# In the last stage, the routing-weight matmul of a unit moves from in front of an older unit's down projection to behind it

## The reference, cut to what matters

```python
shared = silu(xf @ Ws_up) @ Ws_down
w = sigmoid(sel); w = w / (sum(w) + 1e-08)
cw = zeros((T, E)).at[arange(T)[:, None], idx].add(w)
h = silu(einsum('td,edf->etf', xf, W_up))
y = einsum('etf,efd->etd', h, W_down)
routed = einsum('etd,te->td', y, cw)
return shared + routed
```

## Time and profile before

| | us |
|---|---|
| median of 3 runs | 1024.24 |
| lowest and highest run | 1022.57, 1024.37 |
| the profiled execution, whole | 1021.6 |
| its span on the core | 1019.9 |
| TensorE busy in the span | 946.4 (93%) |
| VectorE busy | 825.4 (81%) |
| ScalarE busy | 700.0 (69%) |
| GpSimd busy | 480.2 (47%) |

### The profile page before, as it was taken

The page is one execution under the profiler, slowest core; times in us unless marked ns, Lnnn a source line. Parts: engine busy times, 40 slices in busy tenths (PEclk is TensorE's granted clock), DMA queues, the critical chain, the costliest instruction groups (busy, mean ns, idle before and its releaser), DMA issues.

```text
span 1019.9 us, 20123 instructions
## 1 busy us (share of the span) xinstructions
PE 946.4 (93%) x6082; PEld 754.9 (74%) x6115; DVE 825.4 (81%) x1938; ACT 700.0 (69%) x1394; POOL 480.2 (47%) x550
## 2 busy tenths in 40 slices
PE   3686999999789999999999979999999999999997
PEld 2564998999657677767776657787877777778786
DVE  6888776777778888888887668989898889898865
ACT  3763554555467777877787657777777778777875
POOL 3278782107456565656553404444444444444443
PEclk8765999999779999999999999999999999999999
DMA  8994332222201110110010008493939292939291
GB/s 258 403 386 167 109 95 67 69 66 69 60 24 28 30 29 23 29 33 24 22 32 12 1 16 197 97 210 82 213 76 220 72 222 66 213 76 219 70 228 42
DMA packets 69156, 111.00 MB, mean 109 GB/s; under 512 B 16783, under 2 KB 54706, under 8 KB 64962
## 3 DMA queue, kind: packets, MB, share of 16 engines
q1 hardware_dynamic: 64080, 100.72, 37.8%
q0 software_dynamic: 4384, 8.99, 2.8%
q10 hardware_dynamic: 594, 0.09, 0.0%
HBM read 70.90 MB, written 38.86 MB: 108 GB/s over the span
## 4 chain that ended last, share of the span: by engine, by line
PE 74%; DVE 16%; ACT 4%; issue 3%; DMA 1%; SPq 1%; DVEq 0%; POOLq 0%; ACTq 0%
PE ps L2494 6%; PE ps L2476 5%; PE ps L2477 5%; PE ps L2478 5%; PE ps L2495 5%; PE ps L2496 5%; PE ps L2199 3%; DVE nm L1919 3%; PE ps L2307 3%; PE ps L2329 3%; PE ps L2301 3%; PE ps L2346 3%; PE ps L2177 2%; PE ps L2179 2%; PE ps L2178 2%
## 5 line engine op out<-in xcount | busy, mean ns | idle before, releaser
L927 POOL TENSOR_TENSOR hl<-h,hh 128x512 fp32r<-128x512 f32 x128 | 166.8, 1303 | 247.8 <-ACT hh L1238 247.8
L1238 ACT ACTIVATE hh<-h 128x512 fp32r<-128x512 f32 (+1 forms) x264 | 165.4, 627 | 43.8 <-DVE h L2004 41.2
L2004 DVE TENSOR_TENSOR h<-ps,cwB 128x512 f32<-128x512 f32 x192 | 130.8, 681 | 31.0 <-ACT ps L1227 28.1
L1919 DVE TENSOR_REDUCE nm<-ps 128x4 f32<-128x512 f32 (+1 forms) x128 | 116.3, 951 | 38.0 <-PE ps L2329 35.9
L1227 ACT ACTIVATE ps<-ps 128x512 f32<-128x512 f32 x192 | 111.6, 581 | 25.6 <-PE ps L2478 24.8
L2476 PE MATMUL ps<-xh,wh 128*128 128x512 f32 x256 | 103.0, 403 | 0.0
L2494 PE MATMUL ps<-hh,wh 128*128 128x512 f32 x256 | 102.3, 400 | 0.6 <-POOL hl L927 0.6
L2011 DVE TENSOR_TENSOR hl<-h,hh 128x512 fp32r<-128x512 f32 (+1 forms) x136 | 95.9, 705 | 8.4 <-ACT hh L1238 8.1
L2495 PE MATMUL ps<-hl,wh 128*128 128x512 f32 x256 | 100.0, 390 | 0.0
L2477 PE MATMUL ps<-xl,wh 128*128 128x512 f32 x256 | 100.0, 390 | 0.0
L2478 PE MATMUL ps<-xh,wl 128*128 128x512 f32 x256 | 99.9, 390 | 0.0
(11 more groups left out here) (367 smaller groups left out, 2671.4 us busy)
## 6 DMA issues: line engine op xcount, KB each, us to landing
cwB<-cwd SPq DMA_DIRECT2D x32, 1536.0 KB, 13.8
ys<-zfill SPq DMA_DIRECT2D x13, 1536.0 KB, 22.6
cwd<-cwS SPq DMA_DIRECT2D x64, 96.0 KB
xb<-xs SPq DMA_DIRECT2D x72, 64.0 KB
ys<-yb SPq DMA_DIRECT2D x72, 64.0 KB
x_res<-in_L_attn_x_dram SPq DMA_DIRECT2D x4, 512.0 KB, 6.6
wst<-in_L_ffn_W_up_dram SPq DMA_DIRECT2D x32, 64.0 KB, 2.1
wst<-in_L_ffn_W_down_dram SPq DMA_DIRECT2D x32, 64.0 KB, 1.9
```

Of the source, the lines that this page charges most:

```text
L927: pool.tensor_tensor(hl4[:, slot(u), :], h4[:, slot(u), :], hh4[:, slot(u), :].bitcast(F32), op=ALU.subtract).then_inc(u_hlp, 1)
L1238: act.activation(hh4[r, slot(u), :], h4[r, slot(u), :], ACT.Copy).then_inc(u_hh, 1)
L1919: ins = dve.tensor_reduce(nm[:, u, 4 * g:4 * g + 4], o, axis=AX.X, op=ALU.max, negate=True)
L2004: dve.tensor_tensor(h4[:, slot(u), :], first, second, op=ALU.mult).then_inc(u_h, 1)
```

## The change

The spread matmul is taken out of `e_up` and made a function of its own, which `pe_tile` calls behind the down projection. Nothing else is altered: the same matmuls, the same waits, the same semaphores, in another order on TensorE alone.

```diff
@@ e_up
                 pe.matmul(o, lo, xh4[:, p, :], start=False, stop=True).then_inc(u_up, 1)
+
+            def e_spread(t, p, u):
                 if u > 0 and not broadcast_unit(u):
                     wait_bank(pe, t, "spread", u)
                     pe.matmul(bank[spread_bank(u)][:, :], selr[:, 2 * u - 2:2 * u, :].rearrange("p e f -> p (e f)"), cwT[:, p, :],
                               start=True, stop=True).then_inc(u_cw, 1)
@@ pe_tile
                         e_down(t, p, u - LAG)
                     elif before is not None:
                         e_down(before[0], 1 - p, NU + u - LAG)
+                    e_spread(t, p, u)
                     if before is None:
                         last_attended(u)
```

## The result

| | before | after |
|---|---|---|
| median of 6 runs, us | 1023.57 | 1019.93 |
| lowest and highest, us | 1021.67, 1024.37 | 1019.03, 1020.3 |
| ratio | | 0.9965, 95% interval 0.9954 to 0.9976 |
| profiled execution, us | 1021.6 | 1019.94 |
| its span, us | 1019.9 | 1018.2 |

The kernel became 3.6 us faster; 2.64 us were forecast, and the interval of the ratio (2.5 to 4.7 us of 1023.57) just takes them in. The span of the profiled execution fell by 1.7 us only: its last stage is 2.34 us shorter, but began 0.7 us later (608.67 us into the span against 607.97), behind code that is the same. From here on the spread matmul is L2483 and down is L2496 to L2498, since the edit puts two lines ahead of them.

A forecast was written before the change was run, and what follows sets the result against it. TensorE's row of matmuls in the last stage was taken to bound the kernel; gains of 0.66 + 0.11 + 0.22 + 0.48 + 0.48 + 0.69 = 2.64 us took 1024.24 to 1021.6 us, range 1019.5 to 1024.3.

The forecast's parts named there:

- The holes of unit 6: TensorE's spread matmul there waits for VectorE's late h of unit 4; 0.86, 0.11, 0.22, 0.57, 1.00, 0.57 us in tiles 0 to 5.
- The gain by tile: Last stage, tiles 0 to 5: gains of 0.66, 0.11, 0.22, 0.48, 0.69 and 0.48 us, summing to 2.64 us.
- The 0.09 us of restart kept in tiles 3 and 5: Unit 6: weights load one step ahead only at 769.95, so about 0.09 us stays and each tile gains 0.48 us.
- h at 1.33 us after the last up: Units 1 to 8: h would wait for the moved spread matmul, starting at 1.33 us instead of 1.23, 0.10 later per unit.
- The cap on tile 4: Unit 3's hole closes, but unit 6 arrives 0.63 us earlier at the same late h; tile gains 0.69 us, not 1.63.
- The cover: Units 1 to 8: down comes four units later, so h's 0.10 us delay doesn't add up; without it 6.4 us are lost.
- The loads of the weight rows: Before h of unit 9: the DMA never ended VectorE's idle time, so starting 0.6 us earlier should not find it late.
- The reading by which loads pass the wait: TensorE weight loads passing a waiting spread matmul would leave tiles 3 and 5 no restart; sum 2.82 us.
- VectorE's run of work: Rival: it slips by more than 0.10 us, delaying unit 7 in tiles 0, 3, 4, 5; at 0.3 us, 1022.8 us; chance 0.25.
- The time was not lost again later: Denies the rival that time saved at unit 6 is lost at the tile's next wait; 1024.2 us; chance 0.08.
- VectorE doesn't set the pace in units 1 to 8: Denies the slower rival: each h's 0.10 us adds up, 6.4 us lost and 2.6 gained, 1028.0 us; chance 0.05.
- the rival in which all holes close: Last stage: no restart stays and tile 4's holes close too; gain 3.96 us, time 1020.3 us; chance 0.10.

The follow-up runs named there:

- unit_later: Against the kernel before: each spread matmul goes one whole unit further back, behind the down of the next unit; ratio 1.0013, tiles 1 to 7 357.25 us.
- all_but_six: Against the kernel before: all spread matmuls go behind their down except that of unit 6; ratio 0.9999, tiles 1 to 7 356.60 us.
- stats_late_front: Kernel before, matmul order kept: VectorE's statistics after unit 8 instead of 3, GpSimd's step using them after 9 instead of 5; ratio 0.9965, tiles 1 to 7 354.04 us.
- again: The changed kernel itself measured once more against the kernel before; ratio 0.9966, tiles 1 to 7 354.41 us.
- only_six: Against the kernel before: only the spread matmul of unit 6 goes behind its down; ratio 0.9975, tiles 1 to 7 354.41 us.
- again2: The changed kernel a third time, against the kernel before and beside a control; ratio 0.9966, tiles 1 to 7 354.33 us.
- the version with both edits: Against the kernel before: the changed matmul order and the later statistics together, run twice; ratios 0.9968 and 0.9965, tiles 1 to 7 353.50 and 353.36 us.

## Why the prediction was right, step by step

- *TensorE's row of matmuls sets the time, and a hole comes back in full as length.* Shown. Over all versions, but for `unit_later`, tiles 1 to 6 are 50.1 to 50.3 us plus their holes, and `all_but_six` returned at unit 6 the 0.6 us that it had saved three units earlier.
- *The holes of unit 6 come from h of unit 4, late behind the statistics.* Shown by `stats_late_front`, which closed them without moving a matmul.
- *The gain by tile.* Forecast 0.11, 0.22, 0.48, 0.69, 0.48 for tiles 1 to 5, together 1.98; measured, as differences of the first two profiles, 0.12, 0.21, 0.60, 0.68 and 0.55 (50.73 to 50.18), together 2.16. Tile 0 was forecast at 0.66, and its unit 6 gives about 0.6; its whole length says nothing (50.26 us before, 50.04 after), since the clock at its start differs. The sum counts 60 moved matmuls; it is 61, for only three of tile 0's have no down to pass, and nothing hangs on it.
- *The 0.09 us of restart kept in tiles 3 and 5* was the term that was mis-sized: it is zero. I had h of unit 4 come 0.10 us later. It comes 10.32 us after the start of its tile (769.34 less 759.02), against 10.34 before. That was luck, and not a cover that I had named. h of unit 2 was later, by 0.19 us, and VectorE then worked with hardly a gap in both orders; but the four normalising instructions behind it took 1.83 us and not 2.03, so that h of unit 3 starts 7.39 us into the tile, and 7.41 before. All of the difference is in the first of the four: 1.26 us from 764.32 before, 1.07 us from 764.66 after. In both it ends 0.08 to 0.09 us after GpSimd's hl of unit 1 (765.50 and 765.64), whose place in the tile the change doesn't move; each of the other three takes about 0.26 us. It looks as if VectorE is held there until GpSimd is done, which no run tested.
- *h at 1.33 us after the last up* was 1.42 in tile 3. The row of the silu gives a signal of 0.03 us from TensorE to ScalarE; from the end of the spread matmul to h it is 0.13. It cost nothing in this order, for the reason just given.
- *The cap on tile 4* was right: 0.68 us against 0.69, and 2.12 us still at unit 6.
- *The cover* was named wrongly in part. The delay does not add up from unit to unit, but it isn't the four units to down that bound it; `unit_later` shows the true next limits, `oT` and the logits. At 0.2 us neither is reached, so the sum didn't suffer.
- *The loads of the weight rows* were costed at nothing, with the reason that they never come last. In the profile after they do: VectorE's idle time before h of unit 9 ends with `cwB` in tiles 0, 3 and 7 (1.32, 0.73 and 1.23 us; none in the two profiles of before). In tile 3 h starts 0.82 us after the start of its silu, as it does before, so the load held nothing up; in tiles 0 and 7 it starts 1.38 and 1.28 us after it, against 1.03 and 0.61 in these tiles before. Tile 7 is 52.98 us long all the same, and 52.97 before. `again` and `only_six` have such late loads in two tiles each, `again2` has none. So the cost was right for tile 7 and can't be told for tile 0, and the reason was wrong: the loads now come last at times.
- *The weight load.* The Trainium skill ("TensorE: Matmul & The Clock Gate", Part 2, step-by-step) has loads pulled ahead of matmuls in flight. The traces agree where the wait is over in time (770.09 for 770.32), and not across a wait, where the load starts with its matmul. The reading by which loads pass the wait, 2.82 us, came near the measured sum only because h wasn't late.
- *The rivals.* Tile 4 kept its hole, so not all of them closed. VectorE's run of work slipped by nothing, not by 0.3, though h of unit 2 slipped by 0.19. The time was not lost again later, and VectorE doesn't set the pace in units 1 to 8, not even with h 1.6 us later, which cost 2.9 us against the change and not tens.
- *The size against the runs.* The timed gain of 3.6 us lies outside the 1.8 to 3.3 that the forecast gave itself, and nearer to the 3.96 of the rival in which all holes close; by the time alone one would have picked that rival, and only tile 4's hole rules it out. The time of 1019.93 us is at the lower end of the range of 1019.5 to 1024.3. The forecast of 1021.6 was 1.7 us above it. Of that, 0.7 is the median of before, which fell from 1024.24 to 1023.57 with more runs, and 0.2 is the sum of the holes; the other 0.8 is the difference between timed runs and profiles that stays open, as said.

## What to carry to other kernels

When an engine stops at a wait and ready work of its own stands behind it, put that work in front: the gain is at most the length of what is moved (here 0.68 us a tile), and at most the hole. A hole that is closed in front of a later wait for the same late engine comes back there, as that of unit 3 of tile 4 did at unit 6. Look for the late engine's extra work that makes them, since moving that (here the statistics) closes them as well and can do more. And before deferring an instruction further, follow its consumers through their in-order queues: what suffered here were the transposes of the old tile, behind a copy, and the routing logits of the next, neither of which uses the deferred value.

## What the runs showed of the hardware that I had not expected

- A stop of TensorE costs 0.11 us more than the wait: a matmul behind it follows after 0.34 us where 0.23 is usual, because the weight load waits too. Tile 1 lost 0.12 us to such a stop, which isn't among TensorE's waits in the view; the weight load of the same matmul shows it.
- VectorE stands still for 2.68 to 2.74 us at the start of tile 4, the loop's second pass, in all eleven profiles (until 814.21 before, 813.76 after). In tile 2 the same instruction waits 0.78 us, for hh; here hh was done by 812.23 us, 2 us before VectorE went on. That it is the jump back is an inference from the place. Together with the statistics it makes tile 4 a microsecond longer than its neighbours in the changed kernel (51.20 against 50.15); with the statistics moved it costs next to nothing (50.23).
- The kernel before took 1023 us in some sets of runs and 1086 to 1087 in others, on another chip; the change and the version with both edits, profiled on both chips, had tiles 1 to 7 of the last stage within 0.14 us.
